# Turning 36 of 128 attention rows by an ordinary f32 product, and moving the second layer's first norm into the first layer

## The reference

```python
xn = _layernorm(x)
x = x + attention_0(xn) + soft_mixture_of_experts_0(xn)
xn = _layernorm(x)
x = x + attention_1(xn) + routed_experts_1(xn)
```

```python
scores = (q @ k.T + q_rope @ k_rope.T) / sqrt(HD + D_R)
w = softmax(where(causal, -inf, scores))
attn = (w @ v).reshape(B, T, 128) @ W_o
```

## Time and profile before

| | |
|---|---|
| median of 3 runs | 2899.64 us (2898.55 to 2900.82) |
| the profiled execution, its own time | 2899.65 us |
| its span, first to last instruction | 2897.9 us |
| TensorE, VectorE, ScalarE, POOL busy | 2779.1, 2408.1, 2077.1, 1534.6 us |
| layer 0 / layer 1 | up to 1076 us / from 1076 us |

### The profile page before, as it was taken

One profiled execution on the slowest core, in us unless ns is written; L12 is line 12 of the kernel. 1 busy time (PEld: TensorE's weight loads), 2 busy tenths in 40 slices (PEclk: granted clock), 3 DMA queues, 4 the chain that ended last, 5 costly groups with the idle time before them and its releaser, 6 DMA issues.

```text
span 2897.9 us, 71219 instructions
## 1 busy us (share of the span) xinstructions
PE 2779.1 (96%) x27076; PEld 1597.5 (55%) x27076; DVE 2408.1 (83%) x4452; ACT 2077.1 (72%) x4411; POOL 1534.6 (53%) x1355
## 2 busy tenths in 40 slices
PE   5999999999999978999999999999999999999997
PEld 3656665655556544555555555555555555555554
DVE  6888888888878758888888888888888988888886
ACT  3777777777777776777677777777767777777764
POOL 2333333433333344666666666666666666666664
PEclk8999999999999998999999999999999999999999
DMA  4222222222222234445445455454555455454452
GB/s 133 56 59 75 65 67 57 62 63 56 64 74 65 60 100 121 114 112 149 108 122 142 110 127 129 125 126 123 118 134 128 106 135 127 116 136 117 116 146 70
DMA packets 272083, 298.10 MB, mean 103 GB/s; under 512 B 30848, under 2 KB 235648, under 8 KB 271488
## 3 DMA queue, kind: packets, MB, share of 16 engines
q1 hardware_dynamic: 247424, 274.70, 37.9%
q10 hardware_dynamic: 24320, 18.85, 2.0%
HBM read 141.39 MB, written 25.69 MB: 58 GB/s over the span
## 4 chain that ended last, share of the span: by engine, by line
PE 50%; DVE 7%; issue 3%; ACT 1%; POOL 0%; DMA 0%; ACTq 0%; POOLq 0%; SPq 0%; DVEq 0%
PE l_ps_out L1706 8%; PE l_ps_any L1595 6%; PE l_ps_any L1597 5%; PE l_ps_any L1596 5%; PE l_ps_any L1743 5%; PE l_ps_exp L1687 4%; PE l_ps_exp L1689 4%; PE l_ps_any L1752 4%; PE l_ps_any L1662 4%; PE l_ps_sum L1728 3%; PE l_ps_exp L1691 2%; PE l_ps_any L1667 1%; DVE l_q_lo L1423 1%; PE l_ps_any L1589 1%; DVE l_yT L1536 1%
## 5 line engine op out<-in xcount | busy, mean ns | idle before, releaser
L1271 POOL TENSOR_TENSOR stage<-l_p_in,stage 128x512 f16<-128x512 f32 x640 | 758.8, 1197 | 406.5 <-ACT l_p_in L1384 405.5
L1380 ACT ACTIVATE stage<-l_ps_exp 128x512 f16<-128x512 f32 x640 | 389.1, 608 | 158.6 <-PE l_ps_exp L1691 137.7
L696 DVE TENSOR_REDUCE neg_max<-ps_any 128x1 f32<-128x384 f32 (+3 forms) x704 | 407.3, 636 | 100.9 <-PE ps_any L825 96.7
L1280 POOL TENSOR_TENSOR l_hid<-l_hid,l_spread 128x512 f32<-128x512 f32 x256 | 340.6, 1336 | 243.8 <-DVE l_hid L1549 213.1
L469 POOL TENSOR_SCALAR_AFFINE_SELECT probs<-probs 128x512 f32<-128x512 f32 x256 | 162.1, 648 | 463.8 <-ACT probs L556 415.3
L556 ACT ACTIVATE probs<-ps_exp 128x512 f32<-128x512 f32 x640 | 348.2, 601 | 71.0 <-PE ps_exp L840 66.4
L1384 ACT ACTIVATE l_p_in<-l_ps_exp 128x512 f32<-128x512 f32 x640 | 391.8, 612 | 0.0
L1516 DVE TENSOR_REDUCE l_neg_max<-l_ps_any 128x2 f32<-128x768 f32 (+2 forms) x384 | 310.8, 863 | 17.3 <-PE l_ps_any L1667 14.1
L1687 PE MATMUL l_ps_exp<-l_q_a,l_k_a 128*128 128x512 f16 (+3 forms) x1024 | 305.0, 300 | 3.1 <-DMA l_q_b<-l_max_row 1.6
L1689 PE MATMUL l_ps_exp<-l_q_b,l_k_b 66*128 66x512 f16 (+3 forms) x1024 | 295.4, 300 | 0.0
L823 PE MATMUL ps_any<-k_st,q_st 120*128 120x128 f16 (+3 forms) x1024 | 248.1, 305 | 19.3 <-ACT hT L573 6.8
(11 more groups left out here) (262 smaller groups left out, 6670.1 us busy)
## 6 DMA issues: line engine op xcount, KB each, us to landing
l_spread<-route_scratch SPq DMA_DIRECT2D x128, 512.0 KB, 4.9
l_q_a<-l_q_hi SPq DMA_DIRECT2D x256, 128.0 KB, 2.4
l_y_rec<-rec_scratch SPq DMA_DIRECT2D x128, 256.0 KB, 4.5
l_q_b<-l_q_lo SPq DMA_DIRECT2D x128, 128.0 KB, 2.4
l_k_a<-l_k_hi SPq DMA_DIRECT2D x128, 128.0 KB, 2.7
l_k_a<-l_k_lo SPq DMA_DIRECT2D x128, 128.0 KB, 2.8
l_k_b<-l_k_hi SPq DMA_DIRECT2D x128, 128.0 KB, 2.6
q_st<-rot_hi SPq DMA_DIRECT2D x64, 128.0 KB
```

What stands on the lines that cost most here:

```text
L696: nc.vector.tensor_reduce(neg_max[:, n % 2, heads[0]:heads[0] + k, t], src, AX.X, ALU.max, negate=True).then_inc(drained["dve"], 1)
L1271: nc.gpsimd.tensor_tensor(probs[:, n % 2, 1, u], p_in[:, m % P_SLOTS], probs[:, n % 2, 0, u], ALU.subtract).then_inc(p_lo_ok.sem, 1)
L1280: nc.gpsimd.tensor_tensor(at, at, spread[:, c % 3, n % SPREAD], ALU.mult).then_inc(weighted.sem, 1)
L1380: nc.scalar.activation(probs[:, n % 2, 0, u], bank, ACT.Exp, scale=float(HD1) ** -0.5).then_inc(exp_done.sem, 1)
```

## The change

Four edits:

1. `turn_rows` is a plain f32 product: stationary `y_un` block (128x128), moving the 36 columns of the identity that pick 9 of each 32 rows. VectorE reads the same places as before.
2. The norm and the scaling of layer 1's first batch become steps of layer 0's last batch: `first_norm` ahead of `combine` 0, `first_scale` behind `combine` 3 and ahead of `attnT`. Their tiles and semaphores move to `Early`.
3. In layer 1 the bf16 casts go from VectorE to POOL, ahead of POOL's memsets; ScalarE rounds three weights ahead of the steps and the other two (w_kvu, w_g) behind the copy of `xnT`, and VectorE's low parts follow; TensorE's waits on weights are split accordingly.
4. The DMAs of `late_loads` are issued by SP and not by ScalarE.

```diff
+    last = steps.index(("combine", batches - 1, 0))
+    after = steps.index(("combine", batches - 1, 3)) + 1
+    return (steps[:last] + [("first_norm", batches - 1, 0)] + steps[last:after] + [("first_scale", batches - 1, 0)]
+            + steps[after:])
...
                 if name == "turn_rows":
                     pe.wait_ge(pv_read.sem, pv_read.at(G * b + n, 1))
-                    turned(f"turn_rows{b}_{n}", [y_un[:, t * P:t * P + P] for t in range(TB)])
+                    rows = ident[:].rearrange("p (s c) -> p s c", c=DR)[:, :, 0:HD0 + 1]
+                    out = bank(f"turn_rows{b}_{n}").rearrange("p (t s c) -> p t s c", t=TB, s=G)[:, :, :, 0:HD0 + 1]
+                    for t in range(TB):
+                        ins = pe.matmul(out[:, t], y_un[:, t * P:t * P + P], rows, start=True, stop=True)
+                    ins.then_inc(filled, 1)
...
+                if name == "first_scale":
+                    act.wait_ge(early.stats_ok.sem, early.stats_ok.at(0, 2 * TB + 2))
+                    for t in range(TB):
+                        nc.scalar.activation(early.x_in[:, t], early.x_in[:, t], ACT.Identity, bias=early.shift[:, t:t + 1],
+                                             scale=early.rstd[:, t:t + 1]).then_inc(early.xn_ok.sem, 1)
...
         @block.sync
         def _(sp):
+            for parts, sem in zip(late_loads, (up_loaded, down_loaded, out_loaded)):
+                for dst, src in parts:
+                    sp.dma_start(dst, src).then_inc(sem, 16)
...
-            pool.wait_ge(prep_pool, 1)
-            pool.wait_ge(prep_pool, 1)
+            pool.wait_ge(early.loaded, early.all)
+            nc.gpsimd.tensor_copy(ident_h[:], ident[:]).then_inc(cast_ok, 1)
+            nc.gpsimd.tensor_copy(later_h[:], masks[:, 0:2]).then_inc(cast_ok, 1)
+            nc.gpsimd.tensor_copy(mask_h[:], masks[:, 2]).then_inc(cast_ok, 1)
+            pool.wait_ge(cast_ok, 3)
+            for r in range(2):
+                rows = slice(HD1 * r, HD1 * r + HD1)
+                nc.gpsimd.tensor_copy(ident_2[rows], ident[rows, rows]).then_inc(cast_ok, 1)
+            pool.wait_ge(cast_ok, 5)
+            nc.gpsimd.memset(k_b[HD1:P], SHIFT).then_inc(prep_pool, 1)
+            nc.gpsimd.memset(q_b[HD1:P], P_SHIFT).then_inc(prep_pool, 1)
...
-            for parts, sem in zip(late_loads, (up_loaded, down_loaded, out_loaded)):
-                for dst, src in parts:
-                    act.dma_start(dst, src).then_inc(sem, 16)
             act.wait_ge(early.loaded, early.all)
...
-            high_weights(split_in[:4])
+            high_weights(split_in[:3])
...
+                if name == "xnT" and b == 0:
+                    high_weights(split_in[3:])
...
-                if name == "xnT" and b == 0:
-                    low_weights(split_in[3:4], 3)
-                    casts()
-                if name == "gate" and b == 0:
-                    low_weights(split_in[4:], 4)
...
+                if name == "xnT" and b == 0:
+                    low_weights(split_in[3:], 3)
```

More of the change, by code:

```diff
@@ L170, in layer0_program @@
     first = min(steps.index(x) for x in (("logits_s", 0, 0), ("logits_c", 0, 0)))
-    return steps[:first - 8] + [("snT", 0, 0)] + steps[first - 8:]
+    steps = steps[:first - 8] + [("snT", 0, 0)] + steps[first - 8:]
+    last = steps.index(("combine", batches - 1, 0))
+    after = steps.index(("combine", batches - 1, 3)) + 1
+    return (steps[:last] + [("first_norm", batches - 1, 0)] + steps[last:after] + [("first_scale", batches - 1, 0)]
+            + steps[after:])
 def filled_by0(step):
@@ L639, in _ @@
                                                 ALU.mult).then_inc(xn_ok.sem, 1)
+                if name == "first_norm":
+                    dve.wait_ge(early.x_loaded.sem, early.x_loaded.at(0, 16))
+                    for t in range(TB):
+                        nc.vector.bn_stats(early.stats[:, t], early.x_in[:, t]).then_inc(early.stats_ok.sem, 1)
+                    dve.wait_ge(early.stats_ok.sem, early.stats_ok.at(0, TB))
+                    release(dve, dve_passed)
+                    for t in range(TB):
+                        nc.vector.bn_aggr(early.mv[:, t], early.stats[:, t]).then_inc(early.stats_ok.sem, 1)
+                    dve.wait_ge(early.stats_ok.sem, early.stats_ok.at(0, 2 * TB))
+                    nc.vector.tensor_scalar(early.var_eps[:], early.mv[:, :, 1], EPS, None, ALU.add
+                                            ).then_inc(early.stats_ok.sem, 1)
+                if name == "first_scale":
+                    dve.wait_ge(early.rstd_ok.sem, early.rstd_ok.at(0, 1))
+                    nc.vector.scalar_tensor_tensor(out=early.shift[:], in0=early.mv[:, :, 0], scalar=-1.0,
+                                                   in1=early.rstd[:], op0=ALU.mult, op1=ALU.mult
+                                                   ).then_inc(early.stats_ok.sem, 1)
                 if name == "square":
@@ L1257, in _ @@
                 n = step[2] if len(step) > 2 else 0
-                if name == "norm":
+                if name == "norm" and b:
                     pool.wait_ge(stats_ok.sem, stats_ok.at(b, 2 * TB + 1))
                     nc.gpsimd.tensor_tensor(rstd[:], var_eps[:], neg_half[:], ALU.pow).then_inc(rstd_ok.sem, 1)
[L1261 to L1265, removed]
                 if name == "exp":
@@ L1403, in _ @@
                 nc.vector.memset(ones_in[:, j, j:j + 1], 1.0).then_inc(prep, 1)
-            def casts():
-                nc.vector.tensor_copy(ident_h[:], ident[:]).then_inc(prep, 1)
-                nc.vector.tensor_copy(later_h[:], masks[:, 0:2]).then_inc(prep, 1)
-                nc.vector.tensor_copy(mask_h[:], masks[:, 2]).then_inc(prep, 1)
-                for r in range(2):
-                    rows = slice(HD1 * r, HD1 * r + HD1)
-                    nc.vector.tensor_copy(ident_2[rows], ident[rows, rows]).then_inc(prep, 1)
             def low_weights(parts, first):
@@ L1480, in _ @@
                     low_weights(split_in[:3], 0)
-                if name == "scale":
+                if name == "scale" and b:
                     dve.wait_ge(rstd_ok.sem, rstd_ok.at(b, 1))
@@ L1618, in _ @@
                 if name in ("lat", "gate", "qk") and b == 0:
-                    pe.wait_ge(weights_lo, len(split_in) - 1)
+                    pe.wait_ge(weights_lo, 3)
+                if b == 0 and (name == "v" or name == "qk" and step[3] >= 2):
+                    pe.wait_ge(weights_lo, 4)
                 if name == "max" and step[1:] == (0, 0, 0):
-                    pe.wait_ge(prep, 11)
+                    pe.wait_ge(prep, 6)
+                    pe.wait_ge(cast_ok, 5)
                     pe.wait_ge(prep_pool, 3)
```

29 lines of the change are left out of this document (18 added, 11 removed).

## The result

The changed kernel takes 2914.79 us (median of 4 runs, 2913.8 to 2919.19) against 2899.41 us for the kernel before beside it (4 runs): +15.4 us, ratio 1.0054, 95% interval 1.0039 to 1.0069. Measured a second time it was 2911.69 us against 2897.83, ratio 1.0052 (1.0039 to 1.0066). It is slower, and the forecast of 2924 us was 9 us too high.

A forecast was written before the change was run, and what follows sets the result against it. TensorE's queue of matrix products was taken to bound the first layer (busy 938.5 of 960 us). +28.5 us for turn_rows and -4.0 for the border, +24.5 on 2899.65 us, gave 2924 us; range 2903 to 2932.

The forecast's parts named there:

- The form, two loads a product: turn_rows: each plain f32 product is two passes with a load each; 512 load records of about 190 ns, not 256 of 140.
- rival 1: turn_rows: columns set the pace, loads overlap fully; step 0.25 us, -12 us, -16 with the border, 2884 us; chance 0.08.
- rival 2: turn_rows: loads run at the transpose's pace, 0.49 us a step; +3.2 us, 2899 us in all; chance 0.07.
- rival 4: turn_rows: nothing overlaps, 152 ns a pass, 1.22 us a step; 2940 us in all; chance 0.06.
- The step, 0.97 us: turn_rows: eight passes at step v's 121 ns take 0.97 us instead of 0.44, 0.53 us extra a step.
- part 1: The turn_rows edit: 64 longer steps add +33.9 us before hiding, +28.5 us after it.
- The part absorbed, 5.4 us: First layer: a quarter of TensorE's 21.5 us of idle time absorbs 5.4 us of the longer turn_rows steps.
- Rival 3: First layer: waits swallow all of TensorE's visible idle time, leaving +12.4 - 4.0 = +8.4 us, 2908 us; chance 0.15.
- The border, -4.0 us: Layer border: second layer's routing starts 5.1 us sooner, w_o's product in the first gives back 1.1 us; -4.0 us.

The follow-up runs named there:

- turn_rows alone: The kernel before with only the turn_rows edit (plain f32 product, 36 moving columns): 2918.71 us, ratio 1.0076.
- transposes twice: The kernel before with the four transposes of each turn_rows step issued twice into the same bank: 2919.47 us, ratio 1.0076.
- product, 128 columns: The kernel before with turn_rows as a plain f32 product moving all 128 identity columns: 2922.32 us, ratio 1.0085.
- product twice: The kernel before with turn_rows as the 36-column product, issued twice in each step (16 passes): 2966.87 us, ratio 1.0241.
- border part alone: The whole change without its turn_rows edit, so four transposes as before: 2889.7 us, ratio 0.9962.
- three border kernels: The border part alone (2889.7 us), the same with the scaling behind attnT (2889.06 us), and with norm and scaling left in the second layer (2893.85 us).
- late loads by SP: The kernel before with the five late weight DMAs issued by SP and not ScalarE, nothing else: 2900.18 us, ratio 1.0001.
- the tile of 176 bytes: The kernel before plus an unused tile of 176 bytes a partition, allocated ahead of the first layer's tiles: 2899.96 us, ratio 1.0006.

## Why the prediction was right, and by how much it was off

**The form, two loads a product: right.** 512 load records, 192 ns each where "about 190" was written, and one stationary load for each of two passes a product. It speaks against rival 1 (columns set the pace; it needed a pass under 55 ns) and rival 2 (loads as for a transpose, 61 ns), against rival 4 (152 ns), all by the measured 0.864 us for eight passes.

**The step, 0.97 us: too high, and the largest error of the sum.** It is 0.864 us, so part 1 before hiding is 26.2 us and not 33.9. The price came from v's row as eight passes of 121 ns, "loads with the stream hidden". By the starts of all 16 steps v's passes are not 121 ns apart either: the second starts 184 ns after the first, and the later ones 112 ns apart, exactly as in the new step. So the pace was the same, and the mean over eight mixed it with a first interval that the moving columns do change: 184 ns in v, 164 in the new step with 128 columns, 82 with 36. Those 102 ns are nearly the whole 0.106 us between 0.97 and 0.864. Why v's first interval is 20 ns longer than that of the new step with 128 columns, no run shows. By the Trainium skill, TensorE: Matmul & The Clock Gate, section LDWEIGHTS, a load is its columns over 1.2 GHz, 107 ns for 128 whatever moves. The trace agrees that the moving columns do not set the pace; its loads start 112 ns apart, 5 ns more than the page says. The step of 0.85 us that the prediction worked out from the page is near the 0.864 in part because the first interval of 82 ns makes up for these 5 ns in each of the others.

**The part absorbed, 5.4 us: of the right order, and the runs cannot say it closer.** From the start of the first step to the end of the last, the time outside the steps shrinks by more than 5.4 us in four kernels with longer steps. By the medians of the runs less is missing in the first three:

| kernel | extra step time | at the last attn | rest of the stretch shorter by | by the medians of the runs |
|---|---|---|---|---|
| turn_rows alone | 26.2 | +16.4 | 8.7 | +20.7 |
| transposes twice | 27.9 | +18.2 | 9.4 | +21.5 |
| product, 128 columns | 31.4 | +21.5 | 9.6 | +24.3 |
| product twice | 84.0 | +68.9 | 14.1 | +68.9 |

The kernel before is one execution too, and three executions with the same steps and no gain by their medians have 1.4 to 2.7 us less outside the steps. Against them turn_rows alone absorbed 6 to 7 us. By the medians 5.5 us of its 26.2 are missing at the end of the run, with an interval of some 3.6 us either way. The prediction measured what could absorb by TensorE's idle time, and waits also lie under its records; that was missing from it, and by these figures it is worth 1 to 4 us. Rival 3, that all 21.5 us of idle time absorb, fell: idle time shrank by 5.1 us, and most of the longer steps arrived. The measured time alone would not have told it from the forecast, since it lies between its 2908 us and the forecast's 2924, and a little nearer to 2908.

**The border, -4.0 us: right.** From the last attn to the scores it is -4.2 in both executions of the changed kernel and -4.1 in the border part alone. Inside it the routing is 5.8 us sooner after the layer's start (5.1 was written), and w_o's product, counted from the last attn, 0.9 to 1.0 us late (1.1 was written, and its own figures, 1073.3 - 1072.27, give 1.0): both errors small. POOL's five casts take 0.28 to 0.40 us each, and VectorE is not held by them.

**What was not in it.** Without the longer steps, the kernels with the norm's tiles ahead of the first layer's gain some 6 us there by the medians; beside the longer steps this does not show. A reason that fits is that the waits that it would shorten are filled already, which no run tested. And from the scores to the first yT, 1.4 to 1.8 us come back in three border kernels and in the first profiled execution of the changed kernel, but nothing in its second. In the first, the granted clock there:

```profile
1107.30:1124.40 17.10, 12.16 (x70) 5.40 (x71) 13.85 (x19) 3.58 (x6) 0.00 (x0) 0.50 0.64 155
```

TensorE is busy for 12.2 of 17.1 us at the lower level, 1.2 GHz. Before, the longest such stretch fell on the time in which it mostly waited for weights:

```profile
1076.50:1093.60 17.10, 6.38 (x28) 2.68 (x28) 14.43 (x47) 9.44 (x15) 7.99 (x3) 0.50 0.52 178
```

It is not the border edit as such: kernels without it lose 0.1 to 1.5 us in the same stretch, turn_rows alone the most. What the loss goes with, in all 14 executions, is how long TensorE is busy at the lower level between the scores and the first yT. Where that is 7.9 to 8.5 us, none loses more than 0.1 (before, late loads by SP, the tile of 176 bytes, the changed kernel's second execution); with 8.8 to 9.3 us they lose 0.6 to 1.1, and with 11.6 to 12.5 us, 1.4 to 1.8. I read it as a cost of where the low clock falls; no run moved it on purpose, and what decides where it falls stays open.

**The sum.** The steps cost 26.2 us, of which 20.7 arrive by the medians of turn_rows alone, and the border gives 4.2 back: +16.5; measured +15.4 and +13.9. The forecast was +28.5 - 4.0 = +24.5. Of its excess of 9 us the step's price made 7.7, and what is left, 1.4, is inside the scatter. That its range held is not a sign that the price was right: the range was wide enough for a step priced too high; with the measured step its own working gives 26.2 - 5.4 - 4.0 = +16.8, 2916 us. The profiled execution of the changed kernel, +19.5, has two stretches of 3.4 us at 1.2 GHz with TensorE busy throughout; no other execution is at that level in the middle of a layer:

```profile
233.50:236.90 3.40, 3.40 (x22) 2.12 (x24) 2.63 (x6) 1.44 (x3) 0.92 (x2) 0.50 0.01 2
1598.90:1602.30 3.40, 3.40 (x10) 1.20 (x9) 3.40 (x6) 2.15 (x5) 1.28 (x2) 0.50 0.28 59
```

Between "first yT" and "mid" in the table it loses 1.8 us, and the second execution does not.

## What to carry to other kernels

Before shortening a moving operand, look at what paces the sequence: a plain f32 product of a 128-column stationary tile costs two loads 112 ns apart here, so it cannot come near a transpose's 110 ns, however few columns move. When a price is taken from a row, look at the starts inside it before dividing by the count: here one interval at the front held all that the moving columns cost, and the mean spread it over eight passes. When a queue of products is lengthened, a part vanishes in waits, some of them hidden under records: 6 to 9 of the first 26 us in the traces here, and 5 of the next 58. Split a change into its parts: here one part cost 20.7 us and hid another that was worth 10.4, and the parts' own gains did not add.

## What the runs showed of the hardware

- Ordinary f32 passes with a 128x128 stationary tile start every 112 ns behind the second, with 36 moving columns and with 128. Only the first interval differs, 82 and 164 ns. Their load records last 192 ns. A transpose's lasts 141, and its passes start every 109 to 110 ns.
- POOL casts 128x128 f32 to bf16 in 0.29 us and 128x256 in 0.40, while two memsets of 64x4096 f16 take it 3.51 us each. VectorE's first cast took 2.73 us before, beside such a memset.
- The same DMAs between the same tiles take 61.0, 62.7 or 68.6 ns for a packet of 1024 bytes. An unused tile ahead of them is enough for the step from 62.7 to 68.6, which cost no time.
- From the first scores to the first yT, 36 to 38 us, the 14 executions differ by up to 1.9 us, and the longer ones are those with TensorE busy for 11.6 to 12.5 us of it at 1.2 GHz and not 7.9 to 8.5.
- Two executions of one program differ by 5 us at the end of the first layer (+18.9 and +13.7) with the same steps, and the kernel before and three like it by 2.7: a single trace does not settle a few us there.
